# Far attention tiles turned by VectorE block transposes and DMA instead of TensorE, in a one-core transformer layer

## The reference, cut to what matters

```python
q = q * cos + _rotate_half(q) * sin
k = k * cos + _rotate_half(k) * sin
scores = jnp.einsum('bhqd,bhkd->bhqk', q, k) / math.sqrt(HD)      # HD = 128, s = 1024, H = 16, b = 2
scores = jnp.where(causal[None, None], scores, jnp.finfo(jnp.float32).min)
probs = jax.nn.softmax(scores.astype(jnp.float32), axis=-1).astype(q.dtype)
out = jnp.einsum('bhqk,bhkd->bhqd', probs, v)
out = out.transpose(0, 2, 1, 3).reshape(b, s, H * HD)
return out @ wo + bo
```

## Time and profile before

| | before |
|---|---|
| median of 3 runs | 1116.94 us (1116.71 to 1118.32) |
| span of the profiled execution | 1115.4 us |
| busy: TensorE, VectorE, ScalarE, GpSimd | 99%, 75%, 67%, 57% |
| DMA: bytes, mean share of 16 engines | 56.5 MB, 20% |
| granted TensorE clock, mean | 0.999 |

### The profile page before, as it was taken

One profiled execution on the slowest core, in us unless ns is written; L12 is line 12 of the kernel. 1 busy time (PEld: TensorE's weight loads), 2 busy tenths in 40 slices (PEclk: granted clock), 3 DMA queues, 4 the chain that ended last, 5 costly groups with the idle time before them and its releaser, 6 DMA issues.

```text
span 1115.4 us, 20396 instructions
## 1 busy us (share of the span) xinstructions
PE 1105.2 (99%) x7100; PEld 1006.7 (90%) x7100; DVE 834.9 (75%) x1978; ACT 748.3 (67%) x1584; POOL 638.1 (57%) x516
## 2 busy tenths in 40 slices
PE   9999999999999999999999999999999999999997
PEld 8999899999999999999999999999999999988897
DVE  7776777777777777777777777777777777977776
ACT  5666867666666666666666666666666666688765
POOL 2217666555555555555555555555555556777676
PEclk9999999999999999999999999999999999999999
DMA  5002412121212121212121212121211212230102
GB/s 176 1 1 62 129 39 53 39 62 39 52 39 62 39 53 39 60 39 50 37 60 39 52 39 62 39 48 44 62 38 37 50 40 57 48 110 14 39 1 76
DMA packets 33285, 56.54 MB, mean 51 GB/s; under 512 B 5792, under 2 KB 10016, under 8 KB 33184
## 3 DMA queue, kind: packets, MB, share of 16 engines
q1 hardware_dynamic: 33040, 55.21, 19.9%
q10 hardware_dynamic: 144, 0.03, 0.0%
HBM read 17.47 MB, written 4.19 MB: 19 GB/s over the span
## 4 chain that ended last, share of the span: by engine, by line
PE 95%; POOL 2%; issue 1%; ACT 1%; DMA 1%; DVE 1%; SPq 0%; POOLq 0%; ACTq 0%; DVEq 0%
PE ps_m L458 58%; PE ps_s L458 23%; PE ps_t L608 12%; PE ps_m L505 1%; DMA work<-in_attn_w 0%; POOL acc L2341 0%; POOL qk_lo L2346 0%; PE ps_m L479 0%; POOL wqk_lo L2346 0%; PE ps_t L458 0%; POOL pT_lo L2354 0%; DMA work<-work 0%; POOL acc L2330 0%; PE ps_m L666 0%; PE ps_m L667 0%
## 5 line engine op out<-in xcount | busy, mean ns | idle before, releaser
L2296 POOL TENSOR_TENSOR work<-work,rope 128x512 f32<-128x512 f32 x128 | 165.5, 1293 | 222.8 <-DMA work<-work 222.7
L1784 DVE TENSOR_TENSOR pT_lo<-ps_t,pT_hi 128x512 fp32r<-128x512 f32 (+3 forms) x408 | 210.8, 551 | 32.7 <-ACT pT_hi L1201 30.2
L1201 ACT ACTIVATE pT_hi<-ps_t 128x512 fp32r<-128x512 f32 (+3 forms) x408 | 182.8, 489 | 65.3 <-PE ps_t L608 65.1
L1777 DVE CUSTOM_DVE_ANT_0 ps_s<-ps_s,causal 128x128 f32<-128x128 f32 (+7 forms) x272 | 203.5, 767 | 6.7 <-PE ps_s L458 4.1
L2300 POOL TENSOR_TENSOR work<-work 128x512 f32<-128x512 f32 x128 | 167.6, 1310 | 10.0
L2307 POOL TENSOR_TENSOR qk_lo<-work,qk_hi 128x512 fp32r<-128x512 f32 x128 | 163.0, 1293 | 17.8 <-ACT qk_hi L1158 17.8
L1152 ACT ACTIVATE work<-ps_m,bqk 128x512 f32<-128x512 f32 x128 | 88.8, 694 | 116.5 <-PE ps_m L458 116.4
L1817 DVE SCALAR_TENSOR_TENSOR acc<-ps_m,rinv,acc 128x256 f32<-128x256 f32 x272 | 118.6, 478 | 63.0 <-PE ps_m L458 61.7
L1194 ACT ACTIVATE prob_b<-ps_s,nmax 128x640 f32<-128x640 f32 (+3 forms) x136 | 130.3, 958 | 17.9 <-DVE nmax L1777 14.6
L458 PE MATMUL ps_s<-qk_hi 128*128 128x384 f32 (+5 forms) x384 | 140.6, 366 | 0.0
L1738 DVE SCALAR_TENSOR_TENSOR work<-ps_m,bqk,rope 128x512 f32<-128x512 f32 x128 | 95.5, 746 | 54.3 <-ACT work L1152 54.0
(11 more groups left out here) (235 smaller groups left out, 2822.7 us busy)
## 6 DMA issues: line engine op xcount, KB each, us to landing
work<-work SPq DMA_DIRECT2D x256, 128.0 KB, 2.3
wst<-in_head_qk SPq DMA_DIRECT2D x16, 256.0 KB, 2.9
acc<-in_x_tiles SPq DMA_DIRECT2D x8, 256.0 KB, 6.8
wo_st<-in_L_ffn_wo SPq DMA_DIRECT2D x16, 128.0 KB, 2.4
wst<-in_pair_v SPq DMA_DIRECT2D x8, 256.0 KB, 3.0
x_rows<-acc SPq DMA_DIRECT2D x4, 512.0 KB, 3.6
wst<-in_expert SPq DMA_DIRECT2D x8, 256.0 KB, 3.0
rope<-x_rows SPq DMA_DIRECT2D x4, 512.0 KB, 4.1
```

The lines of the kernel that those rows point to most:

```text
L1201: act.activation(pT_hi[:, slots, cols], t_bank(u, i, j)[:, 0:size * P].rearrange("p (j q) -> p j q", q=P), ACT.Copy).then_inc(t_hi.sem, t_ ...
L1777: dve.tensor_tensor_reduce(s, s, causal[:, T - (i + 1) * P:T], -1.0, ABOVE_ALL, ALU.add, ALU.min, accum_out=nmax[:, u % 2, i:i + 1]).then_ ...
L1784: dve.tensor_tensor(pT_lo[:, slots, cols], t_bank(u, i, j)[:, 0:size * P].rearrange("p (j q) -> p j q", q=P), pT_hi[:, slots, cols].bitcas ...
L2296: pool.tensor_tensor(qs[:, x % 2, :], qs[:, x % 2, :], sin_t[:, c * CH:(c + 1) * CH], ALU.mult).then_inc(sin_done.sem, sin_done.up(u, x))
```

## The change

For the 28 units 3 to 30 the 16 far tiles are no longer turned by TensorE:

- `exponent(u, i)`, i = 4 to 7, is two instructions: far keys and near keys. The far part reads 512 columns in order and writes them so that key k * 4 + g of a tile goes to place g * 32 + k: neighbouring elements go 32 words apart. Its sum goes to `far_sum`; `invert(u, 1)` adds it.
- `turn_far(u, i)`: VectorE transposes the 128 x 512 words in blocks of 32 x 32 within the partitions into `turned` (8 KB a partition, in the memory of `rows` and `hf`).
- `exchange(u)`: SyncE issues four DMAs of 32 partitions x 2048 words to 128 partitions x 512 words, 1 MB in all, into slots 0 to 3 of `pT_lo`. It waits for the last turn and for outputs(u, 0), whose tiles are now in those slots.
- `high_far`, `low_far`: two pieces of 1024 words each on ScalarE (pT_lo to pT_hi) and VectorE (pT_lo minus pT_hi, in place).
- Because the blocks come by query quarter, the near tiles are stored in the same order: runs of 32 words. `outputs(u, 1)` becomes `near_outputs(u)` and `far_outputs(u, 0)`, `far_outputs(u, 1)`, and `high_o`, `low_o` put the columns back in order.
- The lists of `head(u)` are written in another order on TensorE, ScalarE, VectorE and SyncE. GpSimd's is as it was.

The diff, cut to its core (`...` where lines are left out):

```diff
@@ -64,8 +64,22 @@
...
+FAR_UNITS = range(3, LAST - 2)
+FAR = 4 * CH
+Q4 = 32
...
+def is_far(u):
+    return u in FAR_UNITS
...
+def groups_of(u, i):
...
+    return [(1, i - 3)] if is_far(u) and i >= 4 else list(enumerate(TG[i]))
...
@@ -177,8 +191,11 @@
...
+        shared_ln = sb("shared_ln", [P, FAR])
+        rows = shared_ln[:, 0:TC * D].rearrange("p (t d) -> p t d", d=D)
+        hf = shared_ln[:, TC * D:FAR].rearrange("p (k n) -> p k n", n=CH)
+        turned = shared_ln[:, :].rearrange("p (g m i q) -> p g m i q", g=4, m=4, i=4)
+        turned_by_keys = shared_ln[:, :].rearrange("p (g n) -> p g n", g=4)
...
@@ -627,15 +669,38 @@
...
+                early = 4 if c == 0 and not is_far(u) else 0
...
+            def near_outputs(u):
+                s, h = values_of(u) % 2, half_of(u)
+                out = take_bank("pv", u, 1).rearrange("p (g q) -> p g q", g=4)
+                pe.wait_ge(v_lo_done.sem, v_lo_done.at(values_of(u), 3))
+                pe.wait_ge(t_lo.sem, t_lo.at(u, 7, 1))
+                vals = slice(h * HD, (h + 1) * HD)
+                for j in range(TC, NT):
+                    part = (slice(None), slice(None), slice((j - TC) * Q4, P))
+                    high, low = (x[:, j, :].rearrange("p (g q) -> p g q", g=4)[part] for x in (pT_hi, pT_lo))
+                    product(out[part], (v_hi[:, s, j, vals], v_lo[:, s, j, vals]), (high, low), j == TC, False)
+
+            def far_outputs(u, k):
+                s, h = values_of(u) % 2, half_of(u)
+                out = m_bank("pv", u, 1)
+                pe.wait_ge(far_lo.sem, far_lo.at(u, k))
+                vals = slice(h * HD, (h + 1) * HD)
+                for j in (2 * k, 2 * k + 1):
+                    high, low = (x[:, 0:4, j * P:(j + 1) * P] for x in (pT_hi, pT_lo))
+                    last = product(out, (v_hi[:, s, j, vals], v_lo[:, s, j, vals]), (high, low), False, j == TC - 1)
+                if k:
+                    last.then_inc(pv_mm.sem, pv_mm.up(u, 1))
...
@@ -850,29 +915,31 @@
                 transposes(u, 1)
                 scores(u, 5)
                 project_q(n, 0)
+                transposes(u, 2)
                 out_project(u - 1, 1, 0)
-                transposes(u, 2)
+                scores(u, 6)
                 transposes(u, 3)
-                scores(u, 6)
-                out_project(u - 1, 1, 1)
                 project_q(n, 1)
-                outputs(u, 0)
                 transposes(u, 4)
-                project_q(n, 2)
-                out_project(u, 0, 0)
                 scores(u, 7)
                 transposes(u, 5)
-                out_project(u, 0, 1)
+                out_project(u - 1, 1, 1)
+                outputs(u, 0)
+                project_q(n, 2)
+                transposes(u, 6)
+                out_project(u, 0, 0)
+                transposes(u, 7)
                 project_q(n, 3)
                 project_v(v_next, 2 * half_of(u))
                 scores(n, 0)
-                transposes(u, 6)
                 scores(n, 1)
                 scores(n, 2)
+                out_project(u, 0, 1)
                 scores(n, 3)
-                transposes(u, 7)
+                near_outputs(u)
                 project_v(v_next, 2 * half_of(u) + 1)
-                outputs(u, 1)
+                far_outputs(u, 0)
+                far_outputs(u, 1)
...
@@ -1187,27 +1254,39 @@
             def exponent(u, i):
...
+                scores_, to = all_scores[:, score_range(i)], probs(i)
+                if is_far(u) and i >= 4:
+                    act.activation(to[:, 0:CH].rearrange("p (m g k) -> p m k g", g=4, k=Q4),
+                                   scores_[:, 0:CH].rearrange("p (m k g) -> p m k g", g=4, k=Q4), ACT.Exp,
+                                   bias=nmax[:, u % 2, i:i + 1], scale=-1.0, accum_out=far_sum[:, u % 2, i - TC:i - TC + 1])
+                    scores_, to = scores_[:, CH:], to[:, CH:]
+                act.activation(to, scores_, ACT.Exp, bias=nmax[:, u % 2, i:i + 1], scale=-1.0,
                                accum_out=rsum[:, u % 2, i:i + 1]).then_inc(exp_done.sem, exp_done.up(u, i))
...
+            def high_far(u, k):
+                act.wait_ge(exchanged.sem, exchanged.at(u))
+                act.activation(far_part(pT_hi, k), far_part(pT_lo, k).bitcast(F32),
+                               ACT.Copy).then_inc(far_hi.sem, far_hi.up(u, k))
...
@@ -1373,40 +1452,41 @@
...
-                high_p(u, 6)
+                high_p(u, 7)
                 high_values(v_next, 2 * half_of(u))
-                high_p(u, 7)
-                if r == 3:
-                    high_qk_weights(p + 1, 1)
-                    high_o_weights(p + 1, 0)
                 exponent(n, 0)
                 high_qk(n, 2)
+                high_far(u, 0)
+                high_far(u, 1)
                 high_qk(n, 3)
                 exponent(n, 1)
+                high_values(v_next, 2 * half_of(u) + 1)
                 exponent(n, 2)
                 exponent(n, 3)
-                high_values(v_next, 2 * half_of(u) + 1)
                 high_o(u, 1)
                 high_p(n, 0)
                 high_p(n, 1)
...
@@ -1778,20 +1858,37 @@
...
+            def turn_far(u, i):
+                dve.wait_ge(exp_done.sem, exp_done.at(u, i))
...
+                dve.transpose(out=turned[:, :, :, i - 4, :].rearrange("p g m q -> p m g q"),
+                              in_=prob_b[:, i % 2, 0:CH].rearrange("p (m g k) -> p m g k", g=4, k=Q4)).then_inc(turn_done.sem, turn_done.up(u, i))
+
+            def low_far(u, k):
+                dve.wait_ge(far_hi.sem, far_hi.at(u, k))
+                dve.tensor_tensor(far_part(pT_lo, k), far_part(pT_lo, k).bitcast(F32), far_part(pT_hi, k).bitcast(F32),
+                                  ALU.subtract).then_inc(far_lo.sem, far_lo.up(u, k))
...
             def invert(u, c):
                 dve.wait_ge(exp_done.sem, exp_done.at(u, TC * c + TC - 1))
+                if c and is_far(u):
+                    dve.tensor_tensor(rsum[:, u % 2, tiles_of(c)], rsum[:, u % 2, tiles_of(c)], far_sum[:, u % 2, :],
+                                      ALU.add).then_inc(sums_added.sem, sums_added.up(u))
+                    dve.wait_ge(sums_added.sem, sums_added.at(u))
...
@@ -2035,39 +2132,45 @@
                 low_p(u, 0)
                 low_p(u, 1)
                 row_max(u, 5)
+                turn_far(u, 4)
                 rotate(n, 0)
+                accumulate(u - 1, 1, 0)
                 low_p(u, 2)
-                accumulate(u - 1, 1, 0)
+                row_max(u, 6)
+                low_p(u, 3)
+                turn_far(u, 5)
+                rotate(n, 1)
+                row_max(u, 7)
+                low_p(u, 4)
+                accumulate(u - 1, 1, 1)
                 if r == 0:
                     add_value_bias(p, 1)
-                low_p(u, 3)
-                accumulate(u - 1, 1, 1)
                 if r == 2:
                     low_qk_weights(p + 1, 0)
-                rotate(n, 1)
-                row_max(u, 6)
                 invert(u, 0)
+                turn_far(u, 6)
+                turn_far(u, 7)
                 low_o(u, 0)
-                low_p(u, 4)
+                low_p(u, 5)
+                rotate(n, 2)
                 accumulate(u, 0, 0)
-                rotate(n, 2)
-                accumulate(u, 0, 1)
-                row_max(u, 7)
-                low_p(u, 5)
+                rotate(n, 3)
+                low_p(u, 6)
                 row_max(n, 0)
-                low_p(u, 6)
-                rotate(n, 3)
                 low_values(v_next, 2 * half_of(u))
                 low_p(u, 7)
-                row_max(n, 1)
-                row_max(n, 2)
-                row_max(n, 3)
-                low_values(v_next, 2 * half_of(u) + 1)
-                invert(u, 1)
                 if r == 3:
                     low_qk_weights(p + 1, 1)
                     add_value_bias(p + 1, 0)
+                row_max(n, 1)
+                accumulate(u, 0, 1)
+                row_max(n, 2)
+                low_far(u, 0)
+                low_far(u, 1)
+                row_max(n, 3)
+                low_values(v_next, 2 * half_of(u) + 1)
                 low_o(u, 1)
+                invert(u, 1)
 
...
@@ -2556,6 +2659,13 @@
...
+            def exchange(u):
+                sp.wait_ge(turn_done.sem, turn_done.at(u, NT - 1))
+                sp.wait_ge(pv_mm.sem, pv_mm.at(u, 0))
+                for g in range(4):
+                    sp.dma_start(pT_lo[:, g, :].bitcast(F32), turned_by_keys[g * Q4:(g + 1) * Q4, :, :]).then_inc(exchanged.sem, 16)
+                exchanged.up(u)
...
@@ -2647,10 +2757,11 @@
...
                 swap(n, 1)
                 swap(n, 2)
+                exchange(u)
+                swap(n, 3)
                 if r == 2:
                     load_qk_weights(p + 1, 1)
                     load_o_weights(p + 1, 0)
-                swap(n, 3)
```

82 lines of the change are left out of this document (53 added, 29 removed).

## The result

The changed kernel takes 1249.49 us (median of 4 runs, 1246.99 to 1256.54), the kernel before 1117.63 us beside it (4 runs). The ratio is 1.119, with an interval of 1.116 to 1.123. It is slower, as predicted, but by 132 us and not by 72: the time lies 60 us above the forecast of 1189 and 29 us above the upper end of the range. The profiled execution spans 1245.2 us, 129.8 us more than before.

The account below looks back on a forecast made before the run. The prediction took TensorE, 99% busy, to bound the kernel before. After the change, a loop of 13.4 + 2.0 + 8.5 + 5.2 + 1.7 = 30.8 us a unit over 28 units gave 1189 us, range 1085 to 1220.

Parts of the forecast that it names:

- items 1 and 2: From scores(u, 4) to the end of project_q(n, 2), 13.4 us, then to the exchange's first issue, 2.0 us.
- item 3: Exchange and swap(n, 3) on SyncE's queue, from first issue to GpSimd's start: 8.5 us, or 5.6 at the fast rate.
- items 4 and 5: GpSimd's rotation to the end of qk_lo(n, 3), 5.2 us, plus VectorE's far subtractions and GpSimd excluding each other, 1.7 us.
- the loop through queue and GpSimd: Exchange queued ahead of swap(n, 3), which feeds GpSimd's qk_lo(n, 3), which scores(n, 4) awaits: 30.8 us a unit.
- item 1: On TensorE, from scores(u, 4) to the end of project_q(n, 2): 13.4 us, built from one unit's timeline.
- the rival of slow transposes: VectorE's block transposes take 1.3 us each and delay rotate(n, 1): 1217 us, counted into the forecast's upper side.
- the clock: TensorE's granted clock might fall under 1.00 in its new waits, putting the time above the forecast; no size given.
- the floor of 26.4: TensorE's work per unit after 16 transposes leave: 28.2 - 1.8 = 26.4 us.
- the fourth rival: TensorE stays the bound, with a fast exchange and no collision: 1067 up to 1087 us, middle 1078, chance 0.24.
- Charge nothing: ScalarE's exponent writing with a 32-word step, between nothing and a doubling of 0.6 us, was given no cost in time.
- The queue alone: SyncE's queue is the wait but VectorE and GpSimd take turns without loss: 29.1 us a unit, 1141 us, chance 0.12.
- The fast exchange: Exchange and swap(n, 3) take 5.6 us, VectorE and GpSimd collide for 2.3: 28.5 us a unit, 1125 us, chance 0.14.

Follow-up runs that it names:

- one_dma: The changed kernel with only one of the four DMAs of each exchange issued, three query quarters left stale: 1160.82 us.
- few_words: The changed kernel with its two far subtractions run over 8 of 1024 words each: 1197.25 us.
- weights_moved: The changed kernel, nothing left out, with high_o_weights(p, 1) moved behind add_bias(n, 2) and its GpSimd part to the end of the same unit: 1230.05 us.
- bare_order: The changed kernel without turns, exchange, far copies, far subtractions and their waits, and with high_o_weights(p, 1) behind add_bias(n, 2), its GpSimd part later: 1093.23 us.
- x_first: The changed kernel, nothing left out, with the exchange issued ahead of swap(n, 2) in SyncE's queue: 1307.16 us.
- x_late: The changed kernel, nothing left out, with the exchange behind swap(n, 3) in SyncE's queue and far copies and subtractions moved back to suit: 1310.89 us.
- warm: The changed kernel with 12 small unread products on TensorE ahead of the far products, where it waits: 1242.57 us.
- bare: The changed kernel without turns, exchange, far copies, far subtractions and their waits, keeping the new lists, split exponents and short-run products: 1114.19 us.
- bare_unit_step: The changed kernel without turns, exchange, far copies, far subtractions and their waits, the far exponent piece writing its words one behind the other: 1111.22 us.
- turn_step: The changed kernel, nothing left out, with far exponents written one behind the other and VectorE's transpose reading them with a step of four words: 1244.33 us.

## Why the prediction was right and wrong

The starts of scores(4), of the exchange's first issue and of GpSimd's last rotation, and the end of qk_lo(n, 3), read for each of the 28 units, give the terms of the sum as means:

| us a unit | forecast | change | `one_dma` | `few_words` | `weights_moved` |
|---|---|---|---|---|---|
| items 1 and 2: scores(u, 4) to the first issue | 15.4 | 16.52 | 16.47 | 16.58 | 15.85 |
| item 3: first issue to GpSimd's start | 8.5 | 9.15 | 5.78 | 9.21 | 9.29 |
| items 4 and 5: GpSimd to the end of qk_lo(n, 3) | 6.9 | 6.93 | 6.93 | 5.12 | 6.89 |
| from there to the next scores(4) | 0 | 0.23 | 0.54 | 0.28 | 0.21 |
| unit | 30.8 | 32.83 | 29.72 | 31.19 | 32.24 |

Each of the three experiments moves the term at which it was aimed and nearly nothing else. The mechanism of the prediction, the loop through queue and GpSimd, was right. Wrong was the size of two terms: item 1, which was 1.1 us a unit too small together with item 2, and item 3, too small by 0.65. With the 0.23 at the end that is 2.0 us, 57 us for 28 units, of the 60 that were missing; another 2.5 are what the profiled execution lies under the median.

**Right: the loop, and the prices of the new work on VectorE and ScalarE's copies.** The direction, and the place of the waits. The profile shows what was announced: TensorE at 90%, waits ahead of the far products and of scores(4), 184 GB/s while the exchange flows, GpSimd's start over 8 us after the issue. One sign failed: the exchange was to land within 7.5 us of its first issue. The transposes at 0.70 us and the far copies at 1.05 (2.00 for two) were priced right; the rival of slow transposes falls.

**The step that failed first: item 1, read from one unit and taken for all.** In an undisturbed unit the first issue comes 15.55 us after scores(u, 4) (in the unit shown 13.45 for item 1 and 2.11 for item 2), close to the 15.4 of the sum. In the seven units with r == 0 it comes after 18.20. The prediction listed what the lists do to TensorE's work, but not who waits for out_project(u - 1, 1, 1): high_o_weights(p, 1), with add_bias(n, 1) queued behind it. `weights_moved` brings these units to 15.59, which is 0.65 us over all units, and takes 19.4 us off the time; `bare_order` shows the same with 21.0. A further 0.15 is in every unit, and 0.3 lie in the units with r == 3 (16.0 and more, where TensorE also waits for VectorE's accumulate) and in three units with a low clock, below.

**Too small by 0.65 us a unit: item 3.** On the mean of the 28 units the exchange lands 8.3 us after its first issue (7.8 to 9.6), not 7.1, and GpSimd starts after 9.15, not 8.5. It is tempting to put this down to swap(n, 2), whose 0.26 MB are issued 1.2 us ahead. The runs do not bear that out: in `x_first` the swap before has landed 1.9 us before the exchange's first issue, and the exchange still takes 8.3; in `x_late`, with a swap ahead and none behind, it takes 7.9. What the trace shows is that the first of the four transfers alone lands 3.9 us after its issue (3.8 in `x_first`), while a swap of the same 0.26 MB took 2.9. `one_dma`, with one transfer of 256 KB, has a median of 3.6 (the last row of the view of its issuing line, L2666):

```profile
DMA to landing us min/median/max: 3.5/3.6/5.1
```

The other three follow at 5.4, 6.3 and 8.3 us, 0.79 MB in 4.4 us or 177 GB/s, so the rate was nearly right (the prediction took 187). What was mis-sized is the fixed part, taken from a transfer of another shape (64 partitions to 64, here 32 to 128). Why this shape starts later stays open. swap(n, 3) then lands 0.8 us behind the exchange and not 1.4, which gave half of the error back.

**Right in sum: items 4 and 5.** 5.2 + 1.7 = 6.9; measured 6.93. In the unit shown GpSimd lost 0.8 and 1.0 us to the two subtractions. `few_words` takes 1.8 us off this term. The Trainium skill (SBUF — State Buffer, "Who interferes with whom") has the two engines exclude each other where VectorE has two SBUF inputs; the trace agrees, with 2.29 us against 1.22. That both sides are held up, VectorE's subtractions too (4.25 us for 2.4), and the far products with them, was missing from the sum, but it ends only five units, by at most 0.8 us.

**Named without a price: the clock.** It costs little at the far products, which are seldom last, but it also reaches into item 1. Three units begin after a wait of TensorE for GpSimd of 1.9 us, with a granted clock of 0.71 or 0.72 over the next six, and their first issue comes 17.1 to 17.5 us after scores(u, 4), 1.5 us later than in their like. One of them:

```profile
340.48 0.38 PE L500 MATMUL ps_s<-qk_hi 128*128 128x320 f32 x1 [1.94 <-POOL qk_lo L2410]
```

```profile
340.48:346.50 6.02, 6.02 (x28) 5.54 (x29) 3.79 (x10) 3.37 (x11) 0.00 (x0) 0.72 0.01 3
```

`warm` bounds the whole of it at 7 us, 0.25 a unit.

**Wrong, but without weight here: the floor of 26.4 and the exponent.** A plain unit of `bare` takes 26.99 us (590.81 to 617.80), and TensorE is busy for 26.75 of them. 16 transposes less are therefore worth 28.23 - 26.75 = 1.5 us of TensorE and not 1.8, and 0.24 of these go into the new wait for low_o. The short runs of the products cost nothing, as the prediction took it: the twelve products of four whole tiles take 2.75 us before (505.36 to 508.11) and as far products in `bare` (615.03 to 617.78), and the near ones 1.86 in both (508.11 to 509.97, 611.68 to 613.54). With the 1.2 us that are left the fourth rival's best case would have been 1083, not 1067; the best measured without the chain is 1093, of which the units with r == 3 explain 8 us (1.1 us more than the others, seven times). The exponent piece of 512 words takes 1.22 us and not 0.69, over the 0.8 that the prediction set as proof against its prices. "Charge nothing" was wrong as a price and nearly right for the time: `bare_unit_step` gains 3 us, `turn_step` 5. The Trainium skill (SBUF — State Buffer, "Door 1: The DMA port swizzle", note on cachelines) says that an access which goes to another line of 16 bytes each time pays a penalty. The trace agrees for ScalarE's writes (1.22 us for 0.69) and for VectorE's reads with a step of 16 bytes (1.09 for 0.70). The prediction did not use the rule.

**The rivals.** The queue alone (1141) falls with the exclusion shown. The fast exchange (1125) falls with 184 GB/s. TensorE as the bound falls with both. The range was drawn from these four and had only slow transposes above the forecast; no case took an error in item 1 or in the fixed part of item 3.

## What to carry to other kernels

Before moving a long transfer into a queue, price it from a transfer of its own shape, or from its parts with a bound, and look for the next transfer that feeds the engine which ends the unit: here 1.05 MB in the queue instead of 0.26 cost 3.2 us a unit, more than 16 transposes on TensorE were worth. Read a term over all units before you name the one that was wrong: the single unit shown here would have put 1.3 us on item 3 and 0.2 on items 1 and 2, and the means say 0.65 and 1.1. When an operation moves later on one engine, look up every wait on its event in all units, also in the one of four that does more; one copy of 0.4 us ahead of the wrong neighbour cost 20 us. And put the two-input subtractions of VectorE where GpSimd is idle, or keep one of the operands in PSUM: before, the 408 subtractions of L1784 from PSUM never took more than 0.69 us, with GpSimd busy for 57% of the time.

## What the runs showed of the hardware that was not expected

- VectorE's 32x32 block transpose of 512 words from SBUF to SBUF takes 0.70 us, and 1.09 us when it reads with a step of four words.
- ScalarE's exponent of 512 words from PSUM to SBUF takes 0.69 us, and 1.22 us when it writes with a step of 32 words.
- A subtraction of 8 words, both operands in SBUF, lasts 0.15 us alone and up to 1.31 us beside GpSimd: that is as long as a whole operation of the other engine (1.29), however short it is itself.
- Issues get dearer behind transfers that are still under way. Four of 256 KB took 4.43 us in SyncE's queue, the two small ones behind them 1.35 and 1.62 instead of 0.46 and 0.60, and in ScalarE's queue single ones took 1.18 and 1.98 us, in which that engine's next operation did not start.
- The first 256 KB transfer from 32 to 128 partitions landed 3.8 to 4.0 us after its issue, a swap of 64 to 64 partitions with the same bytes after 2.9; four of them, issued one behind the other in SyncE's queue, after 7.9 to 8.3 on the mean, whether or not a swap was still under way ahead of them.
- After 2.91 us without work TensorE's granted clock was 0.50 in the stretch from 598 to 604 us, and products of 512 columns followed each other in 0.43 us instead of 0.23.
